# Target rows of a message network as runs of 32 table rows through a one-hot matmul, in place of indirect gathers

## The reference, cut to what matters

```
h   = relu(layernorm(x))
z1  = h[src] @ W1[0:128] + h[dst] @ W1[128:256] + edge @ W1[256:320] + b1   # first layer, 256 wide
m   = relu(relu(z1) @ W2 + b2) @ W3 + b3                                     # messages, 128 wide
sum = segment_sum(m, src) + segment_sum(m, dst)
x   = x + mlp3(concat(h, sum, attention))                                    # attention: differences of paired nodes
x   = x + gelu(D^-1/2 (A + I) D^-1/2 (relu(layernorm(x)) @ W) + b)           # D, A: in-degrees and edge counts
```

## Time and profile before

| | us |
|---|---|
| time, median of 3 runs (lowest to highest) | 797.07 (793.92 to 800.56) |
| time of the profiled execution | 798.31 |
| its span in the profile | 796.5 |

### The profile page before, as it was taken

One profiled execution on the slowest core, in us unless ns is written; L12 is line 12 of the kernel. 1 busy time (PEld: TensorE's weight loads), 2 busy tenths in 40 slices (PEclk: granted clock), 3 DMA queues, 4 the chain that ended last, 5 costly groups with the idle time before them and its releaser, 6 DMA issues.

```text
span 796.5 us, 13337 instructions
## 1 busy us (share of the span) xinstructions
PE 762.8 (96%) x4270; PEld 594.8 (75%) x4270; DVE 630.1 (79%) x1453; ACT 482.6 (61%) x642; POOL 554.2 (70%) x530
## 2 busy tenths in 40 slices
PE   4689999999999999999999999999999999997987
PEld 4358777787777787777877777877777877776857
DVE  6988788888888888788888888888888888857654
ACT  3146666667766667666667666667666677653631
POOL 2777777777777777777777777777777777774000
PEclk9789999999999999999999999999999999999999
DMA  6534434444434444334444434444344444331000
GB/s 174 170 113 126 117 114 123 125 122 124 124 111 123 122 124 126 114 119 126 120 126 121 119 117 122 125 126 124 116 117 122 126 120 126 108 118 47 1 0 27
DMA packets 42452, 90.14 MB, mean 113 GB/s; under 512 B 11024, under 2 KB 17808, under 8 KB 42384
## 3 DMA queue, kind: packets, MB, share of 16 engines
q0 software_dynamic: 24576, 67.14, 28.4%
q1 hardware_dynamic: 17808, 22.16, 9.5%
HBM read 86.64 MB, written 2.62 MB: 112 GB/s over the span
## 4 chain that ended last, share of the span: by engine, by line
POOL 67%; issue 20%; PE 7%; DVE 2%; DMA 2%; ACT 1%; DVEq 0%; POOLq 0%
POOL tab_sb L411 34%; POOL tab_sb L419 33%; PE bank L713 2%; PE bank L584 1%; PE bank L672 1%; DMA table_a<-tab_sb 1%; DMA x_sb<-x 1%; PE bank L680 0%; PE bank L666 0%; ACT dist L768 0%; DMA tab_sb<-table_b,ends_i 0%; PE bank L551 0%; DVE oh_key L979 0%; DVE h_sb L867 0%; PE bank L703 0%
## 5 line engine op out<-in xcount | busy, mean ns | idle before, releaser
L411 POOL DMA_INDIRECT tab_sb<-table_a,ends_i x256 | 277.7, 1085 | 79.9 <-issue 77.7
L419 POOL DMA_INDIRECT tab_sb<-table_b,ends_i x256 | 267.0, 1043 | 78.0 <-issue 78.0
L768 ACT ACTIVATE dist<-iota_h,neg_mid 128x1024 f16<-128x1024 f16 x256 | 292.6, 1144 | 0.0
L930 DVE TENSOR_SCALAR inc<-dist,half_gap,times 128x1024 fp32r<-128x1024 f16 x256 | 210.3, 821 | 23.6 <-ACT dist L768 22.7
L762 ACT ACTIVATE h_sb<-bank,b_sb 128x512 f32<-128x512 f32 x128 | 87.5, 684 | 182.4 <-PE bank L563 182.4
L584 PE MATMUL bank<-inc,m_hi 128*128 128x512 f32 x512 | 170.2, 414 | 0.0
L584 PE MATMUL bank<-inc,m_lo 128*128 128x512 f32 x512 | 159.5, 393 | 0.0
L970 DVE TENSOR_TENSOR tab_sb<-tab_sb 128x512 f32<-128x512 f32 x128 | 87.5, 686 | 81.3 <-DMA tab_sb<-table_b,ends_i 81.3
L979 DVE TENSOR_SCALAR oh_key<-iota_h,key_f,minus_base 128x258 bf16<-128x258 f16 x330 | 131.8, 399 | 0.0
L573 PE MATMUL bank<-w_sb,h_sb 128*128 128x128 f32 x1024 | 125.0, 275 | 0.2
L756 ACT ACTIVATE h_hi<-bank 128x512 fp32r<-128x512 f32 x128 | 75.9, 594 | 78.6 <-PE bank L551 78.6
(11 more groups left out here) (162 smaller groups left out, 567.3 us busy)
## 6 DMA issues: line engine op xcount, KB each, us to landing
e_raw<-edge_attr_t SPq DMA_DIRECT2D x128, 128.0 KB, 3.3
tab_sb<-table_a,ends_i POOLq DMA_INDIRECT x256, 3.2
tab_sb<-table_b,ends_i POOLq DMA_INDIRECT x256, 3.0
table_a<-tab_sb SPq DMA_DIRECT2D x1, 1024.0 KB, 4.9
table_b<-tab_sb SPq DMA_DIRECT2D x1, 1024.0 KB, 4.8
x_sb<-x SPq DMA_DIRECT2D x1, 512.0 KB, 4.4
w_sb<-mW SPq DMA_DIRECT2D x2, 256.0 KB, 4.4
out<-oh_key SPq DMA_DIRECT2D x4, 128.0 KB, 1.8
```

Of the source, the lines that this page charges most:

```text
L411: nc.gpsimd.indirect_dma_start(got[:, b, t, 0, :], None, table_a, bass.IndirectOffsetOnAxis(ap=ends_i[:, 0, tile:tile + 1], axis=0),).then ...
L419: nc.gpsimd.indirect_dma_start(got[:, b, t, 1, :], None, table_b, bass.IndirectOffsetOnAxis(ap=ends_i[:, 1, tile:tile + 1], axis=0),).then ...
L768: nc.scalar.activation(dist[:, t, :], iota_h[:, :], ACT.Abs, bias=neg_mid[:, bass.ds(g * GT + t, 1)]).then_inc(dist_ready, 1)
L930: nc.vector.tensor_scalar(inc[:, t, :], dist[:, t, :], half_gap[:, tile], times[:, tile], ALU.is_equal, ALU.mult).then_inc(inc_ready, 1)
```

## The change

- MAIN = 63 groups go through the unrolled loop in a new form. The 64th group, and any group whose targets span more than 32 nodes, goes through a loop with a run-time count, `far_group`, which runs after the others on every engine. On these inputs it is visited once, for group 63.
- Table B is kept as two tables, high half (rounded to fp32r, copied out by ACT) and low half (the rest, by DVE). The bias goes to table A, which DVE now copies out of PSUM.
- Per group, SP reads the group's first target (a register load) and loads 32 consecutive rows of each half of table B into partitions 64 to 127 of `near_raw`; POOL rounds them with one 128 x 256 copy (`near_w`), whose partitions 0 to 63 hold the low half of the edge weights. SP also loads the group's dst row to 64 partitions. POOL's gathers by dst are gone from the main loop; those by src go to a ring of 4 groups.
- Per group ACT rounds the edge attributes to fp32r (`split_edges`), DVE subtracts that on partitions 64 to 127 (`low_edges`) and makes the one-hot of each edge's target in the run (`near_one_hot`, 64 x 512). `add_pairs` is gone.
- PE's first layer (fp32r): two matmuls on all 128 rows (`edge_part`), one pair on array halves (`low_part` k=0, `near_part` k=1), four transposes, a wait for the first pair (half_in), the second pair (`low_part` k=1, `near_part` k=0). The other four transposes as before.
- `far_group`: 12 gathers, two additions of 128 x 1024 on DVE, and the group's layers and scatter one after the other.
- DVE gets a chain for the bases of the runs and the list of far groups ahead of line 1046, and 5 instructions after `middles`.

```diff
+    NEAR = 32
+    MAIN = GROUPS - 1
+    RING = 4
@@ SP
+            def load_near(g):
+                wait(sp, near_ready, g - 1)
+                base = sp.value_load(base_i[0:1, g:g + 1], min_val=0, max_val=N - NEAR)
+                for half, table in enumerate((table_bh, table_bl)):
+                    rows = slice(ED + half * NEAR, ED + (half + 1) * NEAR)
+                    sp.dma_start(near_raw[rows, g % 2, :], table[bass.ds(base, NEAR), :]).then_inc(near_loaded[g % 2], 16)
+            for g in range(MAIN):
+                load_near(g)
+                if g + 2 < MAIN:
+                    sp.wait_ge(e_ready, g + 1)
+                    load_edges(g + 2, g % 2)
+                    load_targets(g + 2, g % 2)
@@ POOL
-                    gather_a(g, t)
-                    gather_b(g, t)
+            for g in range(MAIN):
+                b = g % RING
+                if g >= RING:
+                    pool.wait_ge(z1t_psum, KH * (g - RING + 1))
+                for t in range(GT):
+                    gather_rows(got[:, b, t, :], table_a, ends_i[:, 0, tile:tile + 1], ga_done[b][t])
+                pool.wait_ge(near_loaded[g % 2], 32 * (g // 2 + 1))
+                nc.gpsimd.tensor_copy(near_w[:, g % WINS, :], near_raw[:, g % 2, :]).then_inc(near_ready, 1)
@@ PE
+            def first_layer(g, k):
+                if k == 0:
+                    pe.wait_ge(e_ready, g + 1)
+                    pe.wait_ge(near_ready, g + 1)
+                    wait(pe, h1_lo_ready, 2 * g)
+                    edge_part(g % 2)
+                    low_part(g % 2, g % WINS, 0)
+                    near_part(g % 2, g % WINS, 1).then_inc(half_in, 1)
+                for t in range(GT):
+                    if k == 0:
+                        pe.wait_ge(ga_done[g % RING][t], 16 * (g // RING + 1))
+                    mm = turn_rows(g % RING, t, k)
+                if k == 0:
+                    pe.wait_ge(half_in, g + 1)
+                    low_part(g % 2, g % WINS, 1)
+                    mm = near_part(g % 2, g % WINS, 0)
                 mm.then_inc(z1t_psum, 1)
+            def far_group(v):
+                g = v + MAIN
+                pe.wait_ge(e_ready, g + 1)
+                pe.wait_ge(h1_lo_ready, 2 * g)
+                edge_part(1)
+                low_part(1, 0, 0)
+                low_part(1, 0, 1)
+                pe.wait_ge(far_added, v + 1)
+                for k in range(KH):
+                    for t in range(GT):
+                        mm = turn_rows(3, t, k)
+                    mm.then_inc(z1t_psum, 1)
+                second_layer(g, 1, 0)
+                second_layer(g, 1, 1)
+                messages(g)
+                for t in range(GT):
+                    scatter(g, 1, t)
@@ DVE
-            def add_pairs(g, b, n):
+            def near_one_hot(g, b, n):
+                dve.wait_ge(dst_loaded[b], 16 * (n + 1))
+                wait(dve, z1t_psum, KH * (g - 1))
+                nc.vector.tensor_scalar(near_hot[ED:P, b, :], dst_all[ED:P, b, :], near_f[ED:P, g:g + 1], None, ALU.is_equal)
+            def low_edges(g, b):
+                dve.wait_ge(e_cast, g + 1)
+                nc.vector.tensor_tensor(e_hl[ED:P, b, :], e_raw[ED:P, b, :], e_hl[ED:P, b, :].bitcast(F32),
+                                        ALU.subtract).then_inc(e_ready, 1)
```

More of the change, by code:

```diff
@@ L309, in run_groups @@
         def run_groups(engine, group, start, after=None):
-            for g in range(start, GROUPS + 1):
+            for g in range(start, MAIN + 1):
                 group(g, g % 2, g // 2)
@@ new lines, in load_near @@
+            def load_near(g):
[4 more added lines that the diff above has]
+                    sp.dma_start(near_raw[rows, g % 2, :], table[bass.ds(base, NEAR), :]).then_inc(near_loaded[g % 2], 16)
+            for g in range(2):
+                load_edges(g, g)
+                load_targets(g, g)
@@ new lines, in _ @@
+            sp.wait_ge(tab_a_ready, NC // 2)
+            sp.dma_start(table_a.rearrange("(c p) n -> p c n", p=P), tab_sb).then_inc(tab_a_stored, 16)
+            for pair in range(NC // 2):
+                rows = slice(2 * pair * P, 2 * (pair + 1) * P)
+                for ready, part, table in ((b_hi_ready, b_hi, table_bh), (b_lo_ready, b_lo, table_bl)):
+                    sp.wait_ge(ready, pair + 1)
+                    sp.dma_start(table[rows, :].rearrange("(c p) n -> p c n", p=P),
+                                 part[:, 2 * pair:2 * pair + 2, :].bitcast(F32)).then_inc(b_stored, 16)
@@ L658, in _ @@
             pe.wait_ge(rows_ready, 2)
-            run_groups(pe, group, FIRST + 1, {LAST_W + 1: count_ends})
+            run_groups(pe, group, FIRST, {LAST_W + 1: count_ends})
+            pe.wait_ge(far_ready, 1)
+            visits = pe.value_load(far_i[0:1, 0:1], min_val=1, max_val=GROUPS)
+            with pe.Fori(0, visits) as v:
+                far_group(v)
             add_bias_of_sums()
@@ L790, in group @@
                     relu_first(g + 1, 1 - b, 1)
+                if exists(g + 2):
+                    act.wait_ge(e_loaded[b], 32 * (i + 2))
+                    wait(act, z1t_psum, KH * (g + 1))
+                    split_edges(b)
                 if now:
@@ L796, in group, with far_group @@
                     window_out(i + 1)
+            def far_group(v):
+                g = v + MAIN
+                act.wait_ge(e_loaded[1], v * 32 + 32 * (MAIN // 2 + 1))
+                act.wait_ge(z1t_psum, KH * g)
+                split_edges(1)
+                at = act.value_load(far_i[0:1, bass.ds(v + 1, 1)], min_val=0, max_val=GROUPS - 1)
+                for t in range(GT):
+                    distance(g, t, at * GT + t)
+                act.wait_ge(z2_psum, KH * g)
+                for k in range(KH):
+                    act.wait_ge(z1t_psum, KH * g + (k + 1))
+                    nc.scalar.activation(h1_hi[:, 1, k, :], z1t_bank[k][:, :], ACT.Relu).then_inc(h1_hi_ready, 1)
+                relu_second(g, 0)
+                relu_second(g, 1)
+                act.wait_ge(scattered, GT * g)
+                high_messages(g, 1)
             def window_out(w):
@@ L812, in _ @@
             act.wait_ge(mids_ready, 1)
-            run_groups(act, group, FIRST + 1)
+            run_groups(act, group, FIRST)
+            act.wait_ge(far_ready, 1)
+            visits = act.value_load(far_i[0:1, 0:1], min_val=1, max_val=GROUPS)
+            with act.Fori(0, visits) as v:
+                far_group(v)
             act.wait_ge(sums_ready, 1)
@@ L884, in _ @@
                                                ALU.max, ALU.subtract).then_inc(h_lo_ready, 1)
+            dve.wait_ge(ld_b1, 16)
+            for pair in range(NC // 2):
+                dve.wait_ge(tab_psum, pair + 1)
+                nc.vector.tensor_tensor(tab_sb[:, 2 * pair:2 * pair + 2, :],
+                                        tab_bank[pair][:, :].rearrange("p (c n) -> p c n", c=2),
+                                        b1_all.unsqueeze(1).broadcast_to([P, 2, H]), ALU.add).then_inc(tab_a_ready, 1)
             dve.wait_ge(ld_idx, 32)
@@ L940, in group @@
                     incidence(g - 1, 1)
-                if nxt:
-                    add_pairs(g + 1, 1 - b, i + b)
+                if exists(g + 2):
+                    near_one_hot(g + 2, b, i + 1)
                 if makes:
@@ L954, in group @@
                     low_first(g + 1, 1 - b, 1)
+                if exists(g + 2):
+                    low_edges(g + 2, b)
                 if makes:
@@ L1122, in _ @@
             dve.wait_ge(rows_ready, 2)
-            run_groups(dve, group, FIRST + 1, {LAST_W: more_windows, LAST_W + 1: degrees})
+            run_groups(dve, group, FIRST, {LAST_W: more_windows, LAST_W + 1: degrees})
+            visits = dve.value_load(far_i[0:1, 0:1], min_val=1, max_val=GROUPS)
+            with dve.Fori(0, visits) as v:
+                far_group(v)
             dve.wait_ge(sums_ready, 2)
```

264 lines of the change are left out of this document (175 added, 89 removed).

## The result

The changed kernel took 844.28 us (median of four runs, 843.86 to 846.78) where the kernel before took 797.36 on the same chip (four runs, 793.92 to 800.56): ratio 1.058, 95% interval 1.055 to 1.061. The forecast was 826, with a range of 804 to 848. The profiled execution took 844.42, with a span of 842.7.

The account below looks back on a forecast made before the run. POOL and PE were both taken as full, PE idling only 9.5 us in the loop. Idle gain -9.5, first layer +11.8, start +8.4, end +17.5 gave +28.2 on 798.31: 826.5, stated as 826 us, range 804 to 848.

Parts of the forecast that it names:

- What bounds the kernel: In the old loop: POOL and PE are both full, 11 us of gathers against 10.82 us of matmuls a group.
- the 9.5 us of idle PE: In the loop, group 0 to 62: all the PE idle time that removing gathers could give back, -9.5 us.
- The first layer on halves: PE's first layer in the loop: 0.19 us more a group, +11.8 us for 62 groups.
- 1.41 less 1.21: PE's first layer per group: new sum 1.41 us against old 1.21; the forecast went on with 0.19 more.
- The start: Before PE's first group: table copies 2.8, runs' chain 3.2, behind middles 1.8, group 0's DVE work 1.3; net +8.4 us.
- The end: From group 62's second layer to the bias: 50 us where 32.2 before, group 63 alone, +17.5 us.
- the forecast's own case: Whole kernel: the forecast with the bounds of start and end, 814 to 838 us, chance 0.55.
- Rival 4: In the loop: a new wait, DVE or ACT 0.3 us a group late, 845 us, chance 0.10.
- Rivals 1 and 2: First layer: halves without the extra 0.10 a step, 814 us, chance 0.15; no price for halves, 796 us, chance 0.13.
- rival 3: First layer: pairs on halves don't overlap but go one after the other, +28 more, 854 us, chance 0.07.
- The signs named for each: PE's even group spacing: forecast 10.47 us, Rivals 1 and 2 10.27 and 9.98, rival 3 10.9 and more; Rival 4 waits.

## Why the prediction was right or wrong

**What bounds the kernel: right on the first chip.** PE was nearly as full as POOL, and the 9.5 us of idle PE were all that the gathers held back there: without the gathers by dst the same loop took 668.4 us on another chip, 8.9 less than 677.3. The changed loop shows PE without a hole, and the chain went from POOL to PE. On the other chips the reading of one trace would have failed: the loop of the kernel before took 125 us more there, of which its trace shows nothing.

**The first layer on halves: the term that was mis-sized, 11.8 us for 28.** The forecast read the 0.20 us that two f32 steps cost beyond full matmuls as 0.10 a step. It is 0.20 a visit, the 0.10 and 0.09 at its two ends. Two visits with one pair each pay it twice: 0.46 + 2 x (0.09 + 0.43) + 0.06 + 0.11 = 1.66 us, where before had 1.21: 0.45 a group and not 0.19. The rows of before could not tell the two readings apart, since both give 1.06 for two steps in one visit; they should both have been priced. With the price set per visit the sum would have been some 840 us. (The forecast's own pieces, 1.41 less 1.21, give 0.20 and not the 0.19 that it went on with; that is 0.6 us in all.) The sentence that the change doubles the number of changes of the array's shape was the right thought, without its number. The Trainium skill, "TensorE: Matmul & The Clock Gate", Measured speedup vs the span model, gives about one matmul's duration and 4 ns for two tiles. For a further pair in a visit the runs agree (0.23), for a visit as a whole they don't (0.43).

**A term that was not there: 0.07 us a group.** The matmuls of the second layer start 0.232 us apart where they were 0.227 apart, in every kernel with the loaded runs, also in the one without halves. 4 us in all; its cause was not looked for.

**The start: 9.95 us for 8.4, with errors both ways.** Table A's copies on DVE were priced at 2.8 us and put the chain off by 0.8 (22.69 for 21.92), because DVE had waited for PE there. The bases' chain took 6.1 us and not 3.2: POOL's three weight splits held three small instructions of DVE, and the forecast had looked at those splits only for what they do to PE. The five instructions behind `middles` took 1.8, and `near_one_hot` and `low_edges` 1.2, as said; the first layer of group 0 became 0.1 shorter and not 0.7.

**The end: 12.7 us for 17.5.** The scatter of group 62 ended 25.0 us behind its second layer (24 forecast), but DVE's work for the last group did not queue behind it. The forecast put 3.8 us for the entry of its loop, 1.5 and 3.0 in a row from 22.7 on. In fact DVE made the low half of the last group's edges at 778.84, 21 us behind the start of group 62 and 0.04 behind its last work ahead of the loop, made the incidence rows as PE freed them, and began its additions at 783.87, about when PE was done. The transposes came at 28.7 and not 33. The serial part behind them took 16.2 us, 17 forecast.

**The sum.** In the loop about -9 for the idle time and +28 for the first layer and +4 for the second where +11.8 was forecast (from group 0 to group 62 it is +23.6 in all, and +2.3 was forecast; some 0.6 us of it has no name here). At the start +9.95 for +8.4, at the end +12.7 for +17.5: 46.2 of span for 28.2. The errors of loop and start point up, 21.3 and 1.6 us; that of the end points down and hid 4.8 of them. That 844 lies inside the range is luck to that extent: it is outside the 814 to 838 that the forecast's own case allowed, and with the end as priced it would have been 849, outside the range as well. The direction, slower, and what bounds the kernel were not luck. Rival 4 named 845 us, close to what came, but its mechanism did not occur: nothing waits in the loop. Rivals 1 and 2, cheaper halves, fell at 0.43; rival 3, pairs one after the other, fell at starts less than 10 ns apart and at the lone instruction that cost as much as a pair. The signs named for each were enough to tell them apart: groups 10.80 and 11.92 apart and no wait fit none of them exactly, and that sent the search to the price of a visit.

## What to carry to other kernels

Price work on parts of the array by the changes of shape and not by the instruction (here about 0.19 us a change, 0.15 towards transposes): gather all work on halves into one stretch, or fill the other half with something so that the full array can be used, even at the cost of another engine's copy. When idle time of the bound engine is small, count what the replacement adds to that engine before counting what it frees elsewhere, and price a serial tail for a rare case, since it is paid on every input. And a kernel whose POOL issues gathers without a pause may have a time that does not hold elsewhere: measure it on several chips before trusting a ratio.

## What the hardware showed that was not expected

- One pair of 64-row fp32r matmuls between full-array ones: 0.43 us, one alone on half the array the same 0.43, two pairs 0.66; two full matmuls 0.47. Each change of shape costs some 0.09 us on the instruction before it and 0.10 on the one behind (0.06 on a transpose), and weights are not loaded ahead across it.
- DVE's instructions from SBUF to SBUF on 64 elements a row, normally 0.2 us, ended each with one of POOL's 1.26 us subtractions when these ran beside them (1.03, 1.18, 1.29). With the subtractions cut short they took 0.20, 0.18 and 0.27.
- With gathers issued without a pause, ACT, DVE and PE went on late in 24 of 62 groups on one chip, in none on another; the same kernel took 797 us and 924. Rows a quarter as long by dst changed next to nothing (910.6 for 911.0), a quarter fewer gathers with pauses between them removed it (791.4).
